# Attention part of a graph kernel: fp32 left terms, a scatter of three bfloat16 parts, and gl blocks brought by DMA

## What is computed

```python
h = maximum(layernorm(x), 0)
gl = (h @ Wl.T)[src]; gr = (h @ Wr.T)[dst]             # per pair: 4 heads of 16
score = (att * leaky_relu(gl + gr, 0.2)).sum(-1)       # per pair and head
alpha = softmax of score over the pairs of one src
out = segment_sum(gr * alpha, src)
x = x + gelu(concat(out, h) @ W1.T + b1) @ W2.T + b2
# layer 1: agg = segment_sum(h2[src] + edge_attr, dst), a small network, a batch norm, added to x
```

## Time and profile before

| | |
|---|---|
| median of 3 runs | 9489.05 us (9473.34 to 9510.54) |
| the profiled execution | 9484.91 us, of which span 9483.1 us |
| granted TensorE clock | mean 0.537; 0.50 in the attention part |
| DMA | 557.62 MB, mean 59 GB/s |
| POOL busy | 5015.6 us, 53% of the span |
| DVE, PE, ACT busy | 43%, 39%, 3% |

### The profile page before, as it was taken

How to read it: one execution, slowest core, us unless ns; L and a number is a source line. 1 busy time by engine, 2 the same in 40 slices (tenths; PEclk the granted TensorE clock), 3 DMA queues, 4 the chain that set the end, 5 groups by cost and what they waited for, 6 DMA issues and landing times. The chain is left out here.

```text
span 9483.1 us, 86794 instructions
## 1 busy us (share of the span) xinstructions
PE 3658.2 (39%) x21987; PEld 3222.2 (34%) x21988; DVE 4090.3 (43%) x6783; ACT 260.2 (3%) x352; POOL 5015.6 (53%) x4913
## 2 busy tenths in 40 slices
PE   1011112344444444444444434445463333334445
PEld 1011112343343334343333334334363333333344
DVE  8999823343444343434444344435441122222222
ACT  3011000000000000000000000000010000000000
POOL 0000065656565656556565656565417777676664
PEclk9975555555555555555555555555565555555555
DMA  2000022323232322223232223233711121111111
GB/s 21 0 0 0 26 59 68 80 78 81 69 84 74 79 76 80 72 72 83 67 88 76 77 69 83 75 77 84 66 55 46 43 45 45 44 44 44 43 44 34
DMA packets 442077, 557.62 MB, mean 59 GB/s; under 512 B 172858, under 2 KB 176058, under 8 KB 441698
## 3 DMA queue, kind: packets, MB, share of 16 engines
q1 hardware_dynamic: 281298, 391.72, 13.7%
q0 software_dynamic: 156672, 160.75, 10.8%
q10 hardware_dynamic: 3984, 3.89, 0.2%
HBM read 439.99 MB, written 115.95 MB: 59 GB/s over the span
## 5 line engine op out<-in xcount | busy, mean ns | idle before, releaser
L821 POOL DMA_INDIRECT rows<-gr_table,stage x3328 | 3385.3, 1017 | 3225.4 <-DVE stage L986 2227.2
L1303 POOL DMA_INDIRECT message<-h_table,edge_stage x1568 | 1614.7, 1030 | 783.9 <-issue 466.8
L883 PE MATMUL bank<-terms,hot_sum 128*128 128x68 f32 x6656 | 1610.3, 412 | 777.8 <-issue 753.4
L871 PE MATMUL bank<-gl_parts,hot_t 128*128 x10080 | 953.9, 236 | 2286.5 <-issue 2175.9
L883 PEld LDWEIGHTS bank<-terms,hot_sum 128*128 128x128 f32 x6656 | 1517.7, 326 | 828.8 <-issue 818.2
L871 PEld LDWEIGHTS bank<-gl_parts,hot_t 128*128 128x128 bf16 x10080 | 706.8, 127 | 2549.6 <-issue 2542.5
L1007 DVE TENSOR_TENSOR z<-bank,rows 128x512 f32<-128x512 f32 x416 | 286.6, 689 | 2761.4 <-remote 2618.6
L1330 PE MATMUL bank<-message,edge_hot 128*128 128x64 f32 x3136 | 720.4, 424 | 1463.1 <-DVE message L1375 1368.6
L1330 PEld LDWEIGHTS bank<-message,edge_hot 128*128 128x128 f32 x3136 | 683.5, 330 | 1499.9 <-DVE message L1375 1403.3
L1359 DVE TENSOR_TENSOR agg<-agg,bank 128x64 f32 x196 | 43.4, 221 | 1231.7 <-remote 737.1
L1015 DVE TENSOR_TENSOR hot_sum<-iota_row,place 128x1024 f32<-128x1024 f32 x416 | 506.8, 1218 | 25.7 <-PE bank L883 25.5
(11 more groups left out here) (254 smaller groups left out, 2320.5 us busy)
## 6 DMA issues: line engine op xcount, KB each, us to landing
place_b<-place_rows SPq DMA_DIRECT2D x422, 256.0 KB
gr_rows<-rows SPq DMA_DIRECT2D x416, 256.0 KB
rows_again<-gr_rows SPq DMA_DIRECT2D x416, 256.0 KB
rows<-gr_table,stage POOLq DMA_INDIRECT x3328
edge<-in_edge_attr SPq DMA_DIRECT2D x195, 256.0 KB
message<-h_table,edge_stage POOLq DMA_INDIRECT x1568
pen_s<-pen_rows ACTq DMA_DIRECT2D x56, 64.0 KB
gr_table<-gr SPq DMA_DIRECT2D x1, 1536.0 KB
```

The costliest lines, as they stand in the source:

```text
L821: pool.indirect_dma_start(rows[k][:, g, :], None, m.gr_table[:, :], bass.IndirectOffsetOnAxis(stage[k][:, g:g + 1], 0)).then_inc(s_gath[k] ...
L871: last = pe.matmul(bank[slot][:, g * D:(g + 1) * D], hot_t[slot][:, g * P:(g + 1) * P], m.gl_parts[:, bass.ds(blks[g // GROUP_TILES], 1), ...
L883: last = pe.matmul(sums_of(slot, i), hot2[slot][:, g, :], terms[slot][:, g * HEADS:(g + 1) * HEADS, :].rearrange("p h w -> p (h w)"), star ...
L1303: pool.indirect_dma_start(rows[k][:, e, :], None, m.h2_table[:, :], bass.IndirectOffsetOnAxis(stage[k][:, e:e + 1], 0)).then_inc(s_gath[k] ...
```

## The change

- `hot_t` becomes fp32, and gl stays whole in fp32: a tile's left terms are one fp32 product in place of three of bfloat16. The splitting of gl in `prepare` goes. gl is stored to DRAM as `gl_table`, and SP brings the two blocks of step q + 6 into one of 8 fixed slots `gl_step`, reading the two block numbers into registers (`load_left`). PE reads no block numbers.
- `terms` is split into three bfloat16 parts: ACT copies it (part 0), DVE subtracts (`rest`), ACT copies the rest (part 1), DVE subtracts again (part 2). `hot_sum` becomes bfloat16, and the scatter of a tile is one bfloat16 product with 3 x 68 = 204 columns. `acc` holds the three sums side by side and is added up in `attention_nodes`.
- DVE's order changes: `terms` comes right after `z`, the two additions to `acc` are spread between, `rest` stands ahead of `hot_sum`, the third part behind the stage. PE's step begins with a wait for the third part of step r. Some tiles share memory (`z` and `leaky` with `fore`, `weighed` with `top`), and `terms` has one buffer in place of 4.

```diff
+        m.gl_table = nc.dram_tensor("gl_table", (BLOCKS, P, D), F32).ap()
...
-        m.acc = sb("acc", [P, BLOCKS, HEADS * ACCW], F32)
+        m.acc = sb("acc", [P, BLOCKS, 3, HEADS * ACCW], F32)
         layer0, keys_ctx = (whole.enter_context(ExitStack()) for _ in range(2))
-        m.gl_parts = sb("gl_parts", [P, BLOCKS, 3 * D], BF16, layer0)
...
             store_blocks(sp, m.gr_table, gr, s_grt)
-            sp.wait_ge(s_grt, 32)
+            sp.dma_start(m.gl_table[:, :, :].rearrange("b p f -> p b f"), gl[:, :, :]).then_inc(s_grt, 16)
+            sp.wait_ge(s_grt, 48)
...
-            dve.wait_ge(s_lr, len(rounds))
-
-            for part in range(3):
-                piece = m.gl_parts[:, :, part * D:(part + 1) * D]
-                c.link(dve.tensor_copy(piece, gl[:, :, :]))
-                if part < 2:
-                    c.link(dve.tensor_tensor(gl[:, :, :], gl[:, :, :], piece, ALU.subtract))
...
-    hot_t = [sb(f"hot_t{k}", [P, STEP], BF16, ctx) for k in range(LAG)]
-    hot2 = [sb(f"hot_sum{k}", [P, STEP_TILES, P], F32, ctx) for k in range(LAG)]
-    z = sb("z", [P, STEP_TILES, D], F32, ctx)
-    leaky = sb("leaky", [P, STEP_TILES, D], F32, ctx)
-    weighed = sb("weighed", [P, STEP_TILES, D], F32, ctx)
-    terms = [sb(f"terms{k}", [P, PAIRS, ACCW], F32, ctx) for k in range(LAG)]
+    hot_t = [sb(f"hot_t{k}", [P, STEP], F32, ctx) for k in range(LAG)]
+    gl_s = [sb(f"gl_step{k}", [P, STEP_GROUPS, D], F32, ctx) for k in range(U)]
+    hot2 = [sb(f"hot_sum{k}", [P, STEP_TILES, P], BF16, ctx) for k in range(LAG)]
+    fore = sb("fore", [P, SCAN], F32, ctx)
+    z, leaky = (fore[:, i * SW:(i + 1) * SW].rearrange("p (g f) -> p g f", f=D) for i in range(2))
+    wide = sb("wide", [P, SW + STEP_TILES * HEADS * ACCW], F32, ctx)
+    top = wide[:, 0:SCAN]
+    weighed = wide[:, 0:SW].rearrange("p (g f) -> p g f", f=D)
+    rest = wide[:, SW:].rearrange("p (g w) -> p g w", g=STEP_TILES)
+    terms = sb("terms", [P, PAIRS, ACCW], F32, ctx)
+    parts = [sb(f"parts{k}", [P, STEP_TILES, 3, HEADS * ACCW], BF16, ctx) for k in range(LAG)]
...
-        return bank[4 + slot][:, i * HEADS * ACCW:(i + 1) * HEADS * ACCW]
+        return bank[4 + slot][:, i * 3 * HEADS * ACCW:(i + 1) * 3 * HEADS * ACCW]
+
+    terms_by_tile = terms[:, :, :].rearrange("p (g h) w -> p g (h w)", h=HEADS)
...
+            def load_left(q, slot):
+                for i in range(STEP_GROUPS):
+                    blk = sp.value_load(m.blk_i[0:1, bass.ds(q * STEP_GROUPS + i, 1)], min_val=0, max_val=BLOCKS - 1)
+                    sp.dma_start(gl_s[slot][:, i, :], m.gl_table[bass.ds(blk, 1), :, :].rearrange("b p f -> p (b f)")
+                                 ).then_inc(s_gl[slot], 16)
...
                         load_place(q + LAG + 2, (k + LAG + 2) % V)
+                        load_left(q + LAG + 2, (k + LAG + 2) % U)
                         sp.wait_ge(s_gath[k], (j + 1) * 16 * STEP_TILES)
                         sp.dma_start(m.gr_rows[bass.ds(q, 1), :, :].rearrange("q p f -> p (q f)"),
                                      rows[k][:, :, :].rearrange("p g f -> p (g f)")).then_inc(s_store[k], 16)
...
-            def left(q, slot):
-
-                blks = [pe.value_load(m.blk_i[0:1, bass.ds(q * STEP_GROUPS + i, 1)], min_val=0, max_val=BLOCKS - 1)
-                        for i in range(STEP_GROUPS)]
-                pe.wait_ge(s_hot, q + 1)
-                at_least(pe, s_z, q - LAG + 1)
+            def left(slot, loads):
+
+                pe.wait_ge(s_gl[slot], loads * 16 * STEP_GROUPS)
                 for g in range(STEP_TILES):
-                    for part in range(3):
-                        last = pe.matmul(bank[slot][:, g * D:(g + 1) * D], hot_t[slot][:, g * P:(g + 1) * P],
-                                         m.gl_parts[:, bass.ds(blks[g // GROUP_TILES], 1), part * D:(part + 1) * D
-                                                    ].rearrange("p b f -> p (b f)"),
-                                         start=part == 0, stop=part == 2)
+                    last = pe.matmul(bank[slot % LAG][:, g * D:(g + 1) * D], hot_t[slot % LAG][:, g * P:(g + 1) * P],
+                                     gl_s[slot][:, g // GROUP_TILES, :], start=True, stop=True)
                 return last
 
-            def scatter(r, slot):
-
-                pe.wait_ge(s_terms, r + 1)
-                at_least(pe, s_acc, STEP_GROUPS * (r - LAG + 1))
-                for i in range(STEP_GROUPS):
-                    for g in range(i * GROUP_TILES, (i + 1) * GROUP_TILES):
-                        last = pe.matmul(sums_of(slot, i), hot2[slot][:, g, :],
-                                         terms[slot][:, g * HEADS:(g + 1) * HEADS, :].rearrange("p h w -> p (h w)"),
-                                         start=g % GROUP_TILES == 0, stop=g % GROUP_TILES == GROUP_TILES - 1)
+            def scatter(slot):
+
+                for g in range(STEP_TILES):
+                    last = pe.matmul(sums_of(slot, g // GROUP_TILES), hot2[slot][:, g, :],
+                                     parts[slot][:, g, :, :].rearrange("p w f -> p (w f)"),
+                                     start=g % GROUP_TILES == 0, stop=g % GROUP_TILES == GROUP_TILES - 1)
                 return last
...
             def body(part, j, first):
                 for k in range(U):
                     q = U * j + k
+                    if part.sum:
+                        pe.wait_ge(s_parts, q - CHUNK_STEPS + 1)
+                    else:
+                        pe.wait_ge(s_hot, q + LAG + 1)
                     if part.score:
-                        last = left(q + LAG, k % LAG)
+                        last = left((k + LAG) % U, j + (k + LAG) // U + 1)
                     if part.sum:
-                        last = scatter(q - CHUNK_STEPS, k % LAG)
+                        last = scatter(k % LAG)
                     last.then_inc(s_step, 1)
...
+            def body(part, j, first):
+                if not part.sum:
+                    return
+                for k in range(U):
+                    r = U * j + k - CHUNK_STEPS
+                    act.wait_ge(s_terms, r + 1)
+                    nc.scalar.copy(parts[k % LAG][:, :, 0, :], terms_by_tile).then_inc(s_hi, 1)
+                    act.wait_ge(s_rest, r + 1)
+                    nc.scalar.copy(parts[k % LAG][:, :, 1, :], rest[:, :, :]).then_inc(s_mid, 1)
...
-                sums = m.acc[:, bass.ds(blk, 1), :].rearrange("p b w -> p (b w)")
+                sums = m.acc[:, bass.ds(blk, 1), :, :].rearrange("p b w f -> p (b w f)")
                 at_least(dve, s_acc, STEP_GROUPS * r + i)
                 dve.tensor_tensor(sums, sums, sums_of(slot, i), ALU.add).then_inc(s_acc, 1)
...
                         dve.wait_ge(s_gath[k], (j + 1) * 16 * STEP_TILES)
                         dve.tensor_tensor(z[:, :, :], bank[k % LAG][:, 0:SW].rearrange("p (g f) -> p g f", f=D),
                                           rows[k][:, :, :], ALU.add).then_inc(s_z, 1)
+                    if part.sum:
+                        weight = weights[:, bass.ds(tile, STEP_TILES), :].rearrange("p g h -> p (g h)")
+                        dve.wait_ge(s_load[k % V], place_loads(j - outer, k))
+                        dve.tensor_tensor(terms[:, :, 0:DH],
+                                          rows2[k % V][:, :, :].rearrange("p g (h f) -> p (g h) f", f=DH),
+                                          weight.unsqueeze(2).to_broadcast([P, PAIRS, DH]), ALU.mult)
+                        dve.tensor_copy(terms[:, :, DH:ACCW], weight.unsqueeze(2)).then_inc(s_terms, 1)
+                    if add:
+                        accumulate(r - LAG, k % LAG, 0)
+                    if part.score:
                         hot_of(q + LAG, k % LAG, (k + LAG) % V, place_loads(j, k + LAG))
                         dve.wait_ge(s_z, q + 1)
                         dve.scalar_tensor_tensor(leaky[:, :, :], z[:, :, :], SLOPE, z[:, :, :], ALU.mult,
                                                  ALU.max).then_inc(s_leaky, 1)
+                    if add:
+                        accumulate(r - LAG, k % LAG, 1)
                     if part.sum:
+                        dve.wait_ge(s_hi, r + 1)
+                        dve.tensor_tensor(rest[:, :, :], terms_by_tile, parts[k % LAG][:, :, 0, :], ALU.subtract
+                                          ).then_inc(s_rest, 1)
                         at = m.place[:, bass.ds(r * STEP_TILES, STEP_TILES)].unsqueeze(2).to_broadcast([P, STEP_TILES, P])
                         dve.tensor_tensor(hot2[k % LAG][:, :, :], places, at, ALU.is_equal)
-                        weight = weights[:, bass.ds(tile, STEP_TILES), :].rearrange("p g h -> p (g h)")
-                        dve.wait_ge(s_load[k % V], place_loads(j - outer, k))
-                        dve.tensor_tensor(terms[k % LAG][:, :, 0:DH],
-                                          rows2[k % V][:, :, :].rearrange("p g (h f) -> p (g h) f", f=DH),
```

(19 more changed lines are left out.)

25 lines of the change are left out of this document (13 added, 12 removed).

## The result

The changed kernel takes 9152.49 us in the median (9090.63 to 9173.39), beside 9484.07 us for the kernel before on the same chip: a ratio of 0.9636, with a 95% interval of 0.9584 to 0.9687, so 3.6% faster. I had forecast 9610 us. In two later groups of runs, on two chips, the ratio was 0.9597 and 0.9567.

The account below looks back on a forecast made before the run. POOL's gathers were taken to pace the attention part, with stops from PE's starvation. Terms -31 + 12 + 124 + 25 - 17 + 7 gave +120 us, so 9610 us against the median; range 9180 to 9950.

Parts of the forecast that it names:

- POOL's gather paces, the rest are stops; starvation comes with uninterrupted gathering: Attention part: gathers take 10.6 us a step; PE gets no instructions while POOL gathers; 86 stops make 1262.6 us.
- Run length 4.8 to 5.7 steps, -31 us: Attention part: fewer PE instructions lengthen POOL's runs between stops; 61 stops inside chunks in place of 74, 640 against 671 us.
- theory III: Formed after the experiments: POOL's back-to-back gathers keep the engines' instruction supply from filling; it fills whenever POOL issues nothing.
- Rival 2: Attention part, half-way case: POOL's runs grow to 8 or 10 steps; -163 us, or 9325 us; chance 0.22.
- A stop of 10.5 us: POOL's stops inside chunks: 1.4 us of added DVE work ahead of the stage makes each 10.5 us, from 9.1.
- Twelve chunk ends, +12 us: Stops at chunk ends: the same backlog of four PE steps with dearer additions, +1 us each.
- Gathers +124 us, bounds 0 and 250: POOL's pace: two new DVE subtractions stretch the gathers beside them by 0.33 us a step over 376 steps.
- Tail +25 us: Chunk 13, sums only: DVE's step becomes about 4.2 us, +0.8 us for 32 steps; bounds 0 and +60.
- Node part +7: Node part: two additions of 3332 columns join the chain, about 3.5 us each.
- Preparation -17: Preparation: three casts (10.3 us) and two subtractions (6.8 us) leave DVE's chain, -17 us.
- DVE's step 7.1: Attention part: DVE's step grows from 5.38 to 7.1 us, under POOL's 10.9, so hidden except where POOL stands.
- Rival 3: SP's queue starves as its step grows from about 10 instructions to 23; about 300 us, 9900 us; chance 0.15.

Follow-up runs that it names:

- the long pause: Kernel before with a GpSimd memset of 2048 columns (about 1.9 us) at the head of each POOL step; 9080.1 us, ratio 0.9571.
- the kernel with one part: Changed kernel with only the first of the three bfloat16 parts of terms, without both DVE subtractions and ACT's second copy; 9124.92 us, ratio 0.9634.

## Why the prediction was wrong, point by point

- **POOL's gather paces, the rest are stops; starvation comes with uninterrupted gathering** (diagnosis): right. The kernel with the long pause shows it without any other change. One reading under it was wrong: the gather of 1.91 us lies not beside hot_sum alone, but also beside the operation that follows at once:

```profile
3069.44 0.69 DVE L1018 TENSOR_TENSOR terms<-rows_again,weights 128x512 f32<-128x512 f32 x1
```

  It ends at 3070.13, the gather at 3070.34. That back-to-back operations hold a gather as one stood in the trace of the kernel before.
- **Run length 4.8 to 5.7 steps, -31 us**: this is the step that failed. It came to 15.4 steps and -811 us with the chunk ends. I took it from the first chunk, as if instructions were all. But the first chunk has no sums, so no gathers held up by hot_sum, by theory III the least refill of all. Runs there are 7 to 9 steps in the changed kernel, in later chunks up to 31. That isn't the whole miss: the kernel with one part has gathers held up by hardly more than before, and stops of 835 us, 39 of them longer than 0.8 us, where my sum left about 1240 in 73. Rival 2, the nearest, also counted instructions alone.
- **A stop of 10.5 us**: the 23 stops of the changed kernel under 30 us take 14.0 on average, since up to eight steps are now to be caught up.
- **Twelve chunk ends, +12 us**: only three stops over 30 us are left, 129 us against 591. I had kept PE's backlog at each end by assumption. It was PE's work that made it: with 24 products a step given back all 12 ends return, 597 us.
- **Gathers +124 us, bounds 0 and 250**: +400. Two mistakes. DVE work that had fallen into POOL's stops falls beside gathers once there are none: the long pause shows +142 us for that, with no DVE operation added. And the new operations are back to back with the old: the remaining 258 us, if that share is the same here, are just over my upper bound. The same two subtractions in the kernel before cost 47 us. The Trainium skill (SBUF — State Buffer, Who interferes with whom) infers that an operation with two SBUF inputs doesn't stall descriptor generation, since it takes only the read side of the pair; the row of 2.36 us beside three such operations speaks against it. More deeply, I booked these microseconds as cost alone; on a chip that starves they buy stops, as the kernel with one part shows: 351 us of gathers against 384 of the 811 us of stops. In time that is about even (9124.92 and 9152.49 us, on their own chips).
- **Tail +25 us**: +45 from the last gather to the node part. The step is 3.91 us (hot_sum at 6519.12 and again at 6523.03 us), paced by DVE as forecast (4.2), which is 19 of it; 26 come before the last scan, as up to eight steps have to be worked off there. First the last gather, then POOL's first operation of the node part; it waited 191.65 us in the kernel before:

```profile
6381.00 0.94 POOL L821 DMA_INDIRECT rows<-gr_table,stage  x1 [0.30 <-issue]
6618.08 5.36 POOL L1184 IOTA nodes<- 128x6272 f32 x1 [236.14 <-POOLq L810]
```

- **Node part +7**: +43 in this trace, for the clock, not for the additions. PE's clock was granted at 0.50 (1.2 GHz) all through it, while in the second trace of the changed kernel it rose to 1.00 (2.4 GHz) there:

```profile
6645.00:6665.00 20.00, 20.00 (x55) 9.75 (x54) 1.26 (x3) 4.54 (x8) 0.00 (x0) 0.50 0.00 0
```

```profile
6600.00:6640.00 40.00, 40.00 (x199) 21.95 (x198) 4.22 (x10) 18.04 (x33) 0.00 (x0) 1.00 0.00 1
```

  PE is busy throughout in both, and the same program met both levels. With the clock up, the part is 3 us longer than before.
- **Preparation -17, DVE's step 7.1 (6.8 measured), ACT's copies 0, PE's step even**: right.
- **Rival 3**: its mechanism is there, SP in steps of 0.70 us and DVE in 23 waits of 156.5 us for rows_again, about half the price that I gave it.

On the chip without starvation the terms of the prediction but for the stops (124 + 25 - 17 + 7 = 139 us) are near the estimate for the change there, 8381 - 8218 = 163 us. Neither is a measurement.

## What to carry to other kernels

Where one engine issues software DMAs without a break and others stand with "issue" as their only reason, look for what gives the issuing engine a rest before counting instructions: a deliberate pause on the bottleneck, of 0.66 to 1.8 us a step, was worth 3 to 4%, and what looks like interference may be what keeps the rest fed. An idle time called "issue" is not yet starvation: see first when the input was made. Before a cost is priced from a part of the same kernel, ask which other work that part lacks. And a change that trades work against such an effect has to be timed on several chips: 0.96 in three groups here, and on one chip one half of it alone and variants of the whole with a pause only cost.

## What the runs showed of the hardware

- While GpSimd issues indirect DMAs back to back, starvation meets PE, whose instructions come at multiples of 0.70 us, SP, whose DMA instructions take 0.70 us each, and now and then DVE (0.68 and 1.03 us); ACT's copies start 0.04 us after their input all the same. A pause of GpSimd of 1.8 us in a step of eight gathers removes the stops (1263 to 0 us), one of 1.0 us leaves 738 us.
- PE starves while no code is fetched for it: none of its 31 packets of code starts between 2264 and 6882 us.
- It differs between groups of runs on different chips: the same program spans 8209.7 us in one and 9651.7 us in another.
- A gather beside DVE operations with two SBUF inputs back to back is held until the last ends: 2.36 us where one alone takes 0.94.
- TensorE's granted clock in the node part was 0.50 in one execution of the changed kernel and 1.00 in another, 40 us apart in that part.
